# An attention-plus-ternary-FFN layer: the order of every engine's instructions taken from a walk through a table of estimated times, with k and q projected first

## The reference, cut to what matters

```python
# x: (4, 1024, 512); H = 16 query heads in two maps of DH = 32, KV = 4; T = 1024
q, k, v = x @ Wq, x @ Wk, x @ Wv                # rope on q1, q2, k1, k2
a1 = softmax(q1 @ k1.T * scale + causal)
a2 = softmax(q2 @ k2.T * scale + causal)
out = (a1 - lam * a2) @ v                       # lam: one number, from four small vectors
out = groupnorm(out) * gn_w + gn_b              # over time and the 64 columns of a head
x = layernorm(x + out * (1 - LAMBDA_INIT) @ Wo)
wu, wg, wd = ternary(W_up), ternary(W_gate), ternary(W_down)    # scale = mean |W|
x = layernorm(x + (silu(x @ wu.T) * (x @ wg.T)) @ wd.T)         # 2048 hidden columns
```

## Time and profile before

| | |
|---|---|
| median of three executions | 2461.37 us (2460.24 to 2464.53) |
| the profiled execution | 2459.39 us |
| its span, first to last instruction | 2457.6 us |
| mean granted PE clock | 0.972 of full |
| PE / DVE / ACT / POOL busy | 91% / 73% / 58% / 34% of the span |
| DMA | 256.49 MB, 104 GB/s in the mean |

### The profile page before, as it was taken

The page is one execution under the profiler, slowest core; times in us unless marked ns, Lnnn a source line. Parts: engine busy times, 40 slices in busy tenths (PEclk is TensorE's granted clock), DMA queues, the critical chain, the costliest instruction groups (busy, mean ns, idle before and its releaser), DMA issues.

```text
span 2457.6 us, 40664 instructions
## 1 busy us (share of the span) xinstructions
PE 2243.4 (91%) x13586; PEld 1388.2 (56%) x13586; DVE 1803.3 (73%) x4394; ACT 1418.0 (58%) x3462; POOL 845.0 (34%) x1342
## 2 busy tenths in 40 slices
PE   8688887788999999999998999999999999988999
PEld 4356564555665565656565666665665565643444
DVE  1477888898888788878787878877888888842343
ACT  1278664466666666766565666666666776630221
POOL 2333457664432333323422332423421323220132
PEclk9799999899999999999999999999999999998999
DMA  5766664647451322131832223322632121113000
GB/s 172 214 175 202 173 184 137 186 127 213 148 147 56 83 69 78 49 81 61 240 86 64 71 61 95 108 65 83 188 87 70 44 61 52 35 46 126 1 18 18
DMA packets 257599, 256.49 MB, mean 104 GB/s; under 512 B 31344, under 2 KB 199408, under 8 KB 255216
## 3 DMA queue, kind: packets, MB, share of 16 engines
q1 hardware_dynamic: 244864, 218.16, 31.1%
q10 hardware_dynamic: 12528, 35.73, 4.7%
HBM read 182.53 MB, written 71.30 MB: 103 GB/s over the span
## 4 chain that ended last, share of the span: by engine, by line
PE 70%; DVE 11%; POOL 6%; issue 6%; DMA 3%; ACT 3%; SPq 1%; ACTq 0%; DVEq 0%; POOLq 0%
PE F L774 18%; PE F L761 9%; PE PV L720 9%; PE F L783 8%; PE S L703 8%; PE F L688 7%; PE F L744 6%; DVE e_long L1037 3%; PE F L752 2%; PE PV L723 2%; POOL x_lo L1010 2%; POOL hl L992 1%; DVE e_short L1037 1%; POOL coef L965 1%; DVE t L1071 1%
## 5 line engine op out<-in xcount | busy, mean ns | idle before, releaser
L839 ACT ACTIVATE e_long<-e_long,nmax 128x768 f32<-128x768 f32 (+3 forms) x512 | 505.3, 988 | 303.1 <-DVE nmax L1037 301.6
L1037 DVE CUSTOM_DVE_ANT_0 e_long<-S,mask_b 128x768 f32<-128x768 f32 (+3 forms) x512 | 520.8, 1017 | 107.2 <-PE S L703 105.8
L703 PE MATMUL S<-kstk,qstk 128*128 128x384 f32 (+5 forms) x1536 | 513.8, 408 | 93.0 <-DVE nmax L1037 84.5
L965 POOL TENSOR_SCALAR coef<-lsum,linv,neglam 128x1 f32<-128x1 f32 x512 | 186.9, 365 | 1085.4 <-DVE linv L1122 1084.5
L832 ACT ACTIVATE dt_long<-F 128x512 f32<-128x512 f32 (+3 forms) x512 | 263.7, 515 | 292.7 <-PE F L688 291.2
L1037 DVE CUSTOM_DVE_ANT_0 e_short<-S,mask_b 128x384 f32<-128x384 f32 (+3 forms) x512 | 248.5, 485 | 190.6 <-PE S L703 187.9
L703 PEld LDWEIGHTS S<-kstk,qstk 128*128 128x128 f32 x1536 | 281.0, 202 | 168.2 <-DVE nmax L1037 101.2
L744 PE MATMUL F<-xT,wr 128*128 128x512 f32 x640 | 318.0, 628 | 3.4 <-DVE x_lo L1081 2.3
L1115 DVE SCALAR_TENSOR_TENSOR e_long<-e_long,coef 128x1024 f32<-128x1024 f32 (+3 forms) x256 | 302.7, 1183 | 12.5 <-POOL coef L965 11.3
L839 ACT ACTIVATE e_short<-e_short,nmax 128x384 f32<-128x384 f32 (+3 forms) x512 | 285.3, 557 | 25.1 <-DVE nmax L1037 24.6
L688 PE MATMUL F<-ident,e_long 128*128 128x128 f32 x1664 | 273.0, 278 | 11.9 <-ACT xT L860 5.1
(11 more groups left out here) (99 smaller groups left out, 3247.8 us busy)
## 6 DMA issues: line engine op xcount, KB each, us to landing
qstk<-dq SPq DMA_DIRECT2D x512, 128.0 KB, 3.2
dq<-hl SPq DMA_DIRECT2D x32, 1024.0 KB, 5.0
wr<-in_w_proj ACTq DMA_DIRECT2D x48, 512.0 KB, 4.0
kstk<-dk SPq DMA_DIRECT2D x64, 256.0 KB, 5.5
da<-ra SPq DMA_DIRECT2D x32, 512.0 KB, 2.8
at_sb<-da SPq DMA_DIRECT2D x32, 512.0 KB, 4.3
xs<-in_x ACTq DMA_DIRECT2D x36, 256.0 KB, 3.6
dk<-hl SPq DMA_DIRECT2D x8, 1024.0 KB, 5.1
```

The source lines that it names most:

```text
L703: last = nc.tensor.matmul(slot[:, h, :], qstk[:, duo % 4, 2 * r + m, :].bitcast(F32R), kstk[:, g % 2, m, h * w:(h + 1) * w].bitcast(F32R), ...
L839: nc.scalar.activation(e, e, ACT.Exp, bias=nmax[:, u % 8:u % 8 + 1], scale=-1.0, accum_out=lsum[:, n % 4, m:m + 1]).then_inc(s_exp, 1)
L965: nc.gpsimd.tensor_scalar(coef[:, k % 2:k % 2 + 1], lsum[:, k % 4, 0:1], linv[:, k % 8, 1:2], neglam[:, :], ALU.mult, ALU.mult).then_inc(s ...
L1037: nc.vector.tensor_tensor_reduce(out, slot, mask, -1.0, -NEG, ALU.add, ALU.min, nmax[:, u % 8:u % 8 + 1]).then_inc(s_negmax, 1)
```

## The change: what it does

1. `lay_out()`, `share_banks()` and every loop over numbered steps are gone. `in_order()` walks through the program once at build time. It keeps a clock for each engine, knows for each item what must have ended before (`after`), how long it takes (`takes`), how long a DMA takes to land (`LANDS`), and always lets the engine that can start first take its next item. The list of items that comes out, `ORDER`, is the instruction order of each engine. It also assigns the three F banks. Semaphore waits are as before, with a few more that the free order needs (the `evict` of a step waits for the `values` that last read its buffer; small matmuls into PV wait for the products before them).
2. Head step n may not begin in the walk before the first step's end plus `PACE` x n, with `PACE` = 4.0 us. The chip itself is not held to that; only the order comes from it.
3. k and q0 of both halves are projected first, v later; the first-half rest and the second-half rest of q follow in two passes. That makes 40 `xT` jobs in place of 36.
4. The first four rotations are done by DVE alone (`ROT_FIRST = 4`).
5. The first eight x tiles are loaded by SP at once into the weights' buffer, in place of one after the other by ACT; the rope table is issued second by ACT in place of sixth. The first three V evictions have buffers of their own.
6. The weights are summed in steps 0 to 46 and made ternary in steps 55 to 124, one in three steps, in place of 60 to 107, one in two.

```diff
-PASSES = [(0, 0, ALL[:3]), (0, 1, ALL), (0, 0, ALL[3:])] + [(b, h, ALL) for b in range(1, B) for h in range(2)]
+PASSES = [(0, 0, ("k", "q0")), (0, 1, ("k", "q0", "v")), (0, 0, ("v", "q1", "q2", "q3")), (0, 1, ("q1", "q2", "q3"))] +\
+    [(b, h, ALL) for b in range(1, B) for h in range(2)]
...
-STEP_TIME = (3.2, 4.05, 4.05, 4.0)
+ROT_FIRST = 4
+X_FIRST = 12
...
+ABS_AT = [2 * i for i in range(PREP)]
+TERN_AT = [55 + 3 * i for i in range(PREP)]
+HAND_OVER = {"pe": 0.2, "act": 0.12, "dve": 0.1, "pool": 0.12}
+LANDS = {"load q": 3.1, "load k": 5.5, "load v": 4.5, "store v": 3.9, "store rotated": 5.2, "store a": 3.5, "load a": 4.4,
+         "store out": 2.5, "load wo": 4.0, "load x1": 6.0, "load weight": 4.5, "load x": 3.7, "load w": 4.2, "load first": 2.5}
...
+    if what == "scores":
+        return 0.00043 * width(a) + 0.09
+    if what == "turn":
+        return 0.109 * blocks_of(a, b) + 0.06
+    if what == "values":
+        return 0.22 * (STEPS[heads_of(a)[0]].t + 1) + 0.2
+    if what == "exponent":
+        return 0.29 + 0.00083 * width(a)
+    if what == "minimum":
+        return 0.15 + 0.00105 * width(a)
+    if what == "combine":
+        return 0.22 + 0.00102 * width(a)
+    if what == "factor":
+        return 0.67 if STEPS[a].r else 0.36
...
+FIRST = {"scores": (0, 0.4), "mean": (1, 0.1), "variance": (1, 0.1), "totals": (1, 0.1), "turn": (2, 0.25),
+         "values": (3, 0.2), "fill": (4, 0.0)}
+PACE = 4.0
...
+                if item.what == "scores" and item.a and item.b == 0:
+                    r = max(r, end[ITEM("scores")] + PACE * item.a)
...
+            soon = min(h[0] for h in heads)
+            return min((h for h in heads if h[0] <= soon + FIRST[h[2].what][1]), key=lambda h: (FIRST[h[2].what][0], h[0]))
...
+        soon = min(h[0] for h in heads)
+        return min((h for h in heads if h[0] <= soon + 0.02), key=lambda h: h[1] - AHEAD.get(h[2].what, 0.0))
+
+    while True:
+        picks = [(choose(e), e) for e in STRINGS]
+        picks = [(p[0], e, p) for p, e in picks if p]
+        if not picks:
+            break
+        start, e, (_, _, item, s) = min(picks, key=lambda p: p[0])
+        done = start + takes(item)
+        free[e] = done
+        end[item] = done + (LANDS[what] if what in LANDS else HAND_OVER[e])
+        order[e].append(item)
...
-            for st in range(NST):
+            for what, a, b in ORDER["sp"]:
+                if what == "load first":
+                    sp.dma_start(x_first[:, a, :], x_tiles[a]).then_inc(s_xfirst[a], 16)
...
+                back = n - (6 if n % 2 else 4)
+                if half == 0 and back >= 0:
+                    act.wait_ge(s_pv, STEPS[back].duo + 1)
...
+                    if job.kind == "O" and u < ROT_FIRST:
+                        freed(dve, job)
+                        nc.vector.tensor_tensor(t4[:, 0, :], t4[:, 0, :], t4[:, 2, :], ALU.subtract)
+                        nc.vector.tensor_tensor(t4[:, 1, :], t4[:, 1, :], t4[:, 3, :], ALU.add).then_inc(s_rot, 1)
+                        high_part(u)
+                        dve.wait_ge(s_hi, u + 1)
+                        nc.vector.tensor_tensor(hl[:, 2:4, :], t4[:, 0:2, :], hl[:, 0:2, :], ALU.subtract).then_inc(s_lo, 1)
```

More of the change, by code:

```diff
@@ L121, in mixing_jobs @@
     return out
[L124 to L143, removed]
-STEP_TIME = (3.2, 4.05, 4.05, 4.0)
[L146 to L156, removed]
-    ip = im = 0
[L158 to L174, removed]
-            return True
-        if job.kind == "E" and st < done.get("rotated", -9) + 2:
-            return False
-        pass_of = WLOADS[job.i][0]
-        x = JOB("xT", job.b, job.h, pass_of, 2 * job.j + 1 if job.kind == "V" else 3)
-        return st >= done.get(x, 10 ** 6) + 2
@@ new lines @@
+FIRST = {"scores": (0, 0.4), "mean": (1, 0.1), "variance": (1, 0.1), "totals": (1, 0.1), "turn": (2, 0.25),
+         "values": (3, 0.2), "fill": (4, 0.0)}
+AHEAD = {"minimum": 1.0, "exponent": 1.0, "evict": 1.5, "inverses": 1.0, "factor": 2.0, "reciprocal": 0.8, "combine": 0.6, "empty": 3.0, "copy": 2.0,
+         "sum": -1.5, "ternary": -1.5, "less": -2.0, "rsqrt": 1.0, "product": 0.5, "load q": 2.0}
+NTH = 4
+PACE = 4.0
+READER = {"mean": "spread", "variance": "deviation", "totals": "constants"}
@@ L183, in lay_out, with in_order @@
+def in_order():
+    engine_of = {item: e for e, strings in STRINGS.items() for s in strings for item in s}
+    at = {e: [0] * len(strings) for e, strings in STRINGS.items()}
+    free = {e: 3.0 for e in STRINGS}
+    order = {e: [] for e in STRINGS}
+    end, ready_of, jobs, spot = {}, {}, [], {}
+    bank_free, bank_uses = [0.0] * 3, [0] * 3
+    where = {}
+    current = None
+    small = None
+    ip = im = 0
+    at_128 = None
     due = []
-    for job in reversed(proj):
+    for job in reversed(PROJECTION):
@@ L329, in parts_of, with ready @@
-def parts_of(st):
-    one = len(AT[st]) // 2
-    return one, one + (len(AT[st]) - one + 1) // 2
-JOB_WAIT = 3.5
-TURN_BANK, JOB_BANK = share_banks()
-NTH = 4
-PREP = 24
-ABS_STEP = {4 + 2 * i: i for i in range(PREP)}
-TOTAL_STEP = 54
-NEG_STEP = {60 + 2 * i: i for i in range(PREP)}
-TERN_STEP = {61 + 2 * i: i for i in range(PREP)}
+    def ready(item, e):
+        if item in ready_of:
+            return ready_of[item]
+        r = 0.0
+        for other in after(item):
+            if other not in end:
+                return None
+            r = max(r, end[other] + (0.0 if engine_of.get(other, "pe") == e else 0.0))
+        ready_of[item] = r
+        return r
@@ L347, in layer_kernel @@
+    assert len(jobs) == len(PROJECTION) + len(MIXING)
+    assert all(at[e][s] == len(string) for e, strings in STRINGS.items() for s, string in enumerate(strings))
+    return order, jobs, where
+ORDER, JOBS, BANK_OF = in_order()
+INDEX = {job: k for k, job in enumerate(JOBS)}
 def layer_kernel(nc, x, w_proj, wo, lams_in, gn, w_up, w_gate, w_down, rope, out):
@@ L789, in _ @@
             pe.wait_ge(s_const, N_CONST)
[L790 to L810 removed]
+            made, last_small = 0, None
```

937 lines of the change are left out of this document (549 added, 388 removed).

## The result

| | before | changed |
|---|---|---|
| median of six executions | 2460.80 us (2458.99 to 2464.53) | 2448.88 us (2443.53 to 2452.23) |
| ratio of the times | | 0.9947, 95% interval 0.9933 to 0.9961 |
| the profiled execution: time / span | 2459.39 / 2457.6 us | 2448.30 / 2446.5 us |
| mean granted PE clock | 0.972 | 0.976 |

The account below looks back on a forecast made before the run. PE, busy 2243.4 of 2457.6 us, was taken as the bound, leaving at most 214 us idle to win. Terms 57 + 2054 + 32 + 235.5 = 2378.5 of span, 1.8 outside: 2380 us, range 2343 to 2432.

Parts of the forecast that it names:

- second term: The 511 head steps: all at 4.02 us, 2054 us; gain 20, almost all from steps 52 to 116.
- First term: Time until first scores: k and q first bring them to 57 us (53 to 62), gain 27.
- First to last, one for one: Start to end of span: the start's gain of 27 us was counted fully in the sum.
- rival A: Batch 0's ternary phase stays slow through POOL's delayed coefficient: 4.34 us a step, say 2415 us; chance 0.12.
- Rival D: DVE's queue: DVE stands at emptyings while PE is late, slower than before, 2482 us at 4.22 a step; chance 0.09.
- its sign: Rival D's sign: DVE idle before an `empty` released by PE F in hundreds of cases.
- The balance: PE before step 511: 1978 us of work leaves 133 us idle, 115 needed; 18 us of batch 2's mixing moves ahead.
- Third term: From step 511's scores to batch 3's first `wo`: normalisation no longer stretched by jobs, 32 us, gain 31.
- Fourth term: From batch 3's first `wo` to the end, its mixing: unchanged at 235.5 us.

Follow-up runs that it names:

- early_w: Changed kernel with only SP's list altered: each of the 48 weight tiles issued two q loads (some 8 us) earlier; median 2430.6 us, ratio 0.9876.
- small_w: Changed kernel, order unchanged, weight sums, comparisons and ternary writes on 64 of 1024 columns, so output is not the layer's; median 2414.5 us.
- start_all: Changed kernel with SP's and ACT's first 80 us reordered: fourth rotation's store before k loads, transposed copies before lambda, x1 loads later; median 2447.3 us.
- early_start: early_w with start_all's moves at the start, order otherwise kept; median 2424.2 us.
- fl_start: Changed kernel, walk's weight landing 8.0 us, coefficient 1.0 us longer in steps 0 to 159, plus start_all's moves; median 2393.4 us, ratio 0.9725.
- lands_w8: Changed kernel with the walk's landing time of a weight tile 8.0 us in place of 4.5; median 2418.1 us, ratio 0.9829.
- coef_dve: Changed kernel with weight landing 8.0 us and the coefficient computed on DVE in place of POOL, a new order; median 2425.3 us.
- the twins: Changed kernel with one hand-over estimate moved: PE 0.21 in place of 0.2, or DVE 0.11 in place of 0.1; medians 2419.6 and 2424.1 us.
- v first: v projected ahead of k and q0, three passes (edit 3 undone): on the changed kernel 2427.0 us; with weight landing 8.0 us, 2436.0 us.

## Why the prediction was wrong

The forecast had the direction right and the size wrong. The sum against the profiled execution, term by term: 57, 2054, 32 and 235.5 were forecast; 76.5, 2097.2 (to the scores of step 511 at 2173.7), 38.9 and 233.9 came.

- **The step that failed: the second term in batch 0, 43 us over.** "After, every step is laid out at 4.0 ... I take 4.02 for all 511 steps." Steps 160 to 511 took 3.97 us, 16 us less than forecast. Steps 0 to 160 took 4.38 us, 58 us more. I argued from batches 1 to 3, which "hold such a plan" but have no work on the weights, and from DVE's load. The waits of ACT and POOL for weight tiles stood at nothing, as they were in the kernel before; the changed kernel has 51 us of them. Steps 0 to 128 took 565 us where my figure gives 515. With the tiles issued earlier (early_w) they take 547, with the weights' work nearly gone (small_w) 527. So of the 50 us about 19 are late tiles, and up to another 19 the weights' work itself; the two are not independent. The other 12 stay open.
- **Why the tiles were late.** The trace of before has medians of 5.5 to 6.8 us from issue to landing for the three matrices, against 4.5 in the diff, and I did not compare them. But with 4.8 in the median the 4.5 came out nearly right; what failed is that the plan has no margin behind it, neither for a slow tile nor for a late issue.
- **First term, 19.5 us over.** The first L1071 came at 22.5, not 14: the loads asked for at once landed late (x tiles 9.9 us, for a median of 3.6 before), and ACT stood at lambda. I had named the sharing for the rope table only. The first rotation took 8.0 us in place of 6.3, since DVE waited 2.1 us in it for PE. The others followed 7.9 us apart, as forecast (7.8), but this was luck: I had them wait for the store of the one before, and in the trace they wait for PE's products. That makes 10.6 us. Then came 4.1 us in SP's queue and 6.3 more until the store had landed, less 1.6 for a faster q load. I took this part as now from the earlier trace rows, though the order of SP's issues there was new. start_all shows that 10 of the 19.5 us were order alone.
- **First to last, one for one.** I added the start's gain fully. start_all refutes this for this order; in early_start and fl_start, almost without late tiles, more than half of it comes through.
- **The coefficient, rival A.** Its 4.34 us a step is close to the 4.42 of steps 0 to 128, but its reason is not borne out. In the stretch from 80 to 640 us the mean of the coefficient rose from 0.43 to 0.62 us, which I read as the hold of the earlier trace rows met more often. lands_w8, 31 us faster, has 0.63 there, and small_w, almost without ternary writes, still 0.53; coef_dve took it off POOL and won nothing. (In the earlier trace rows it is POOL that is held up, although its record starts 0.05 us before DVE's.)
- **Rival D** has a trace of its sign. DVE waits for a full PE bank 157 times, 171 us in all, where the kernel before has 65 times and 141 us. From 80 to 640 us the largest group of these waits has 12 us (L1276), and steps 160 to 511 run faster than before, so it is not what slows batch 0; what it costs was not tested.
- **The balance** said that steps and jobs fit. They did: steps 160 to 511 ran 22 us faster than before with all jobs in them. (One of its numbers is off: by its own 1978 us of work the idle before step 511 was 181 us, not 186; the sum does not use it.)
- **Third term, 7 over.** From the scores of step 511 to L1031 it took 14.4 us (14.0 forecast), to L1034 3.6 (1.5), to the store 5.6 (4.5), to `wo` 15.3 (11.0). So the jobs no longer stretch the chain, though L1031 and L1034 are not within 2 us of each other. The largest part is the last one. The first load of the attention was issued 7.4 us behind the store (6.8 before), and `wo` could start 7.9 us behind that issue (4.3 before). I read this as the work of the four loads of x1, which wait for the last outputs and now stand ahead of it; no run moved them. SP in the changed kernel, then that load in the kernel before:

```profile
2192.24 3.69 SPq L840 DMA_DIRECT2D wo_sb<-in_wo  x8
2195.98 0.61 SPq L851 DMA_DIRECT2D out<-x  x1
2197.28 0.33 SPq L822 DMA_DIRECT2D da<-ra  x1
2202.62 1.92 SPq L845 DMA_DIRECT2D x<-in_x  x4
2204.66 16.85 SPq L832 DMA_DIRECT2D at_sb<-da  x3
```
```profile
2217.84 1.00 SPq L601 DMA_DIRECT2D at_sb<-da  x2
```

- **Fourth term** as forecast, within 2 us.
- **Chance.** Of the 69 us, 25 to 29 are this one order: the twins at 2419.6 and 2424.1 lie inside the range I gave. This overlaps with the late tiles above and does not come on top of them. A range for a kernel whose order comes from a greedy walk has to carry that scatter; mine did not. And the twins are still some 40 us above the forecast.

What stays open: which interleaving costs the changed kernel the 7 to 11 us that early_w leaves; why v first helps on one order and harms on another; the 0.12 us a step that batch 0 keeps without the weights' work; and how much of each difference is stalls and how much the lower clock that goes with them (the fastest kernel, fl_start, has a mean granted clock of 0.993, the changed one 0.976).

## What to carry to other kernels

Where engines work strictly in order, everything behind a late tile waits with it. So an order written from estimated times needs a margin between the issue of a load and its first reader, not only a good mean: here 4.5 us against a measured median of 4.8 gave 51 us of waits, and issuing earlier took all of them away although the tiles then landed slower. Before you credit an edit to such a kernel, move one irrelevant estimate by a hair in two runs; here that alone was worth 29 us of 2449, more than most edits. And follow the first store and load of a reordered start through every queue, since a microsecond saved at the front is easily spent behind a transfer issued in front of it.

## What the runs showed of the hardware that I had not expected

Eight x tiles of 256 KB, asked for together on SP beside the weights, the rope table and two small loads on ACT, took 9.9 us to land in the median. In the kernel before, where at most two were asked for at a time, the median over all its 36 was 3.6 us. The 64 KB load for lambda took 10.7 us in the changed kernel, against 5.6.

A rotation's store of 1 MB issued behind eight k loads of 256 KB took 12.5 us to land, with the DMA engines 98% busy. The same store issued ahead of the k loads took 5.6 us in start_all, and 6.3 in the kernel before.
